# A four-block transformer kernel on one core: three moves in a hand-written order of work

## What is computed

```
x = x + wkv(w, u, layernorm(x), context)          # a recurrence over the rows
x = x + ffn(layernorm(x))                         # 8-bit fake-quantised matmul, relu
x = x + attention(layernorm(x), context)          # 16 heads in 8 groups, self and cross, FP8 inputs
x = x + gated_linear_attention(layernorm(x))      # over the 4 batches
```

```
no  = maximum(o, u + k);      A  = exp(o - no);       E  = exp(u + k - no)
y   = (A * p + E * v) / (A * q + E)
no2 = maximum(w + o, k);      A2 = exp(w + o - no2);  E2 = exp(k - no2)
p, q, o = A2 * p + E2 * v,  A2 * q + E2,  no2
```

## Time and profile before

| | |
|---|---|
| median of 3 runs | 672.46 us (672.37 to 672.68) |
| the profiled execution | 672.11 us, span 670.3 us |
| TensorE matmul | 612.7 us busy, 91% |
| TensorE weight loads | 490.7 us, 73% (beside the matmuls) |
| VectorE | 531.5 us, 79% |
| ScalarE | 398.0 us, 59% |
| GpSimd | 256.2 us, 38% |
| mean granted TensorE clock | 0.985 |
| chain that ended last | TensorE 63%, VectorE 20%, issue 7%, GpSimd 5%, ScalarE 4% |

### The profile page before, as it was taken

How to read it: one execution, slowest core, us unless ns; L and a number is a source line. 1 busy time by engine, 2 the same in 40 slices (tenths; PEclk the granted TensorE clock), 3 DMA queues, 4 the chain that set the end, 5 groups by cost and what they waited for, 6 DMA issues and landing times.

```text
span 670.3 us, 13297 instructions
## 1 busy us (share of the span) xinstructions
PE 612.7 (91%) x4567; PEld 490.7 (73%) x4567; DVE 531.5 (79%) x1305; ACT 398.0 (59%) x1339; POOL 256.2 (38%) x338
## 2 busy tenths in 40 slices
PE   4446999999999999999999999999999999999936
PEld 3345787777778787777788877877888888877725
DVE  7998687988887778888777788888664677868697
ACT  4255766666877545667566456575663665554531
POOL 2115664444333544343344443333332444430233
PEclk9997999999999999999999999999999999999978
DMA  8237452442592202322343232232353234020001
GB/s 266 88 151 200 169 166 56 126 156 89 180 334 100 96 22 102 104 103 106 104 124 99 92 103 103 104 104 103 103 168 100 103 103 103 17 33 1 1 0 63
DMA packets 36973, 72.86 MB, mean 109 GB/s; under 512 B 3343, under 2 KB 28587, under 8 KB 32811
## 3 DMA queue, kind: packets, MB, share of 16 engines
q1 hardware_dynamic: 36720, 72.00, 33.4%
q10 hardware_dynamic: 186, 0.02, 0.0%
HBM read 59.41 MB, written 12.60 MB: 107 GB/s over the span
## 4 chain that ended last, share of the span: by engine, by line
PE 63%; DVE 20%; issue 7%; POOL 5%; ACT 4%; DMA 0%; DVEq 0%; POOLq 0%
PE bank L722 13%; PE bank L702 11%; PE bank L591 10%; PE bank L598 6%; PE bank L674 5%; PE bank L746 3%; PE bank L688 3%; PE bank L703 3%; POOL rs L1343 2%; ACT square L1087 2%; DVE nm L1760 2%; DVE Cb L1775 2%; PE bank L832 2%; PE bank L736 1%; PE bank L841 1%
## 5 line engine op out<-in xcount | busy, mean ns | idle before, releaser
L722 PEld LDWEIGHTS bank<-V,Pt 128*128 128x128 f32 x1024 | 128.1, 191 | 28.7 <-DVE Cb L1775 14.9
L1087 ACT ACTIVATE square<-bank 128x128 bf16<-128x128 f32 x372 | 97.9, 280 | 83.8 <-PE bank L591 70.2
L722 PE MATMUL bank<-V,Pt 128*128 128x129 f32 x1024 | 136.3, 276 | 3.0 <-DVE Cb L1775 2.8
L702 PE MATMUL bank<-QT,KTt 128*128 128x512 f32 x256 | 132.6, 599 | 2.2 <-POOL diag L1358 2.2
L1358 POOL TENSOR_TENSOR diag<-identb,nm 128x512 bf16<-128x512 bf16 x64 | 66.9, 1045 | 174.0 <-DVE nm L1760 173.9
L1070 ACT ACTIVATE Pt<-bank 128x512 f32<-128x512 f32 x128 | 76.9, 601 | 64.1 <-PE bank L703 60.9
L1760 DVE TENSOR_REDUCE nm<-bank 128x2 f32<-128x512 f32 x128 | 82.4, 685 | 27.0 <-PE bank L688 26.6
L1343 POOL TENSOR_TENSOR rs<-ve,mhalf 128x6 f32<-128x6 f32 x64 | 90.0, 1406 | 5.3
L1775 DVE SCALAR_TENSOR_TENSOR Cb<-bank,ro,ism 128x128 bf16<-128x128 f32 x256 | 78.1, 347 | 4.5
L591 PE MATMUL bank<-WQ,xq 128*128 128x256 f32 x512 | 79.3, 297 | 1.0 <-DVE xq L1671 1.0
L1087 ACT ACTIVATION_READ_ACCUMULATOR square<-bank 128x1 f32 x372 | 78.1, 210 | 0.0
(11 more groups left out here) (233 smaller groups left out, 1019.8 us busy)
## 6 DMA issues: line engine op xcount, KB each, us to landing
WQ<-wq_split SPq DMA_DIRECT2D x24, 1024.0 KB, 7.8
WH<-wh_split SPq DMA_DIRECT2D x24, 384.0 KB, 8.9
wq_split<-WQ SPq DMA_DIRECT2D x8, 1024.0 KB, 4.5
ism<-smooth_inverse SPq DMA_DIRECT2D x32, 256.0 KB, 6.4
wst<-in_L_xattn_wproj SPq DMA_DIRECT2D x16, 256.0 KB, 4.5
wh_split<-WH SPq DMA_DIRECT2D x8, 384.0 KB, 3.2
wst<-in_L_xattn_wq SPq DMA_DIRECT2D x8, 256.0 KB, 4.6
wst<-in_L_xattn_wqx SPq DMA_DIRECT2D x8, 256.0 KB, 4.8
```

What stands on the lines that cost most here:

```text
L702: nc.tensor.matmul(o[:], KTt[u % 2][:, x, t * P:(t + 1) * P], QT[u % 2][:, x, :], start=True, stop=False)
L722: last = nc.tensor.matmul(o[:, h * (P + 2):h * (P + 2) + P + 1], Pt[:, x, k, h * S + t * P:h * S + (t + 1) * P], V[u % 2][:, x, k, 0:P + 1 ...
L1087: last = A(square[:, t, h], head(t, h), ACT.Square, accum_out=ss[:, t, h:h + 1])
```

## The change

1. VectorE: the two products that make `no` leave `early(b, 1)` and become a step of their own, -1, behind outputs(u, 0, 0) and ahead of normalise(u + 1, 1). It acts in units 0, 8 and 16.
2. TensorE: turn_z of batches 2 and 3 stands behind guard(u + 1, 1) and no longer ahead of it. It acts in units 12 and 20 (in these no weights are transposed at this place).
3. GpSimd: the last output term is a function of its own. For batch 1 it is issued in unit 2 behind diagonals(2, 0), and no longer at the end of unit 1. For batches 2 and 3 it stays where it was.

```
+        SECOND_OF_1 = -1
...
                 if 0 in steps:
                     turn_h(nb)
-                if 6 in steps and b:
-                    turn_z(nb)
                 if u + 1 != G:
                     for r in round_of(u, 2):
                         weights(*r)
                 guard(u + 1, 1)
+                if 6 in steps and b:
+                    turn_z(nb)
...
                 gp.tensor_tensor(E2, E2, Ew, ALU.add).then_inc(s["den_ready"], 1)
                 chain.wait()
+
+            def last_output_term(b):
+
                 gp.tensor_tensor(A2, Aw, PX[:, :, 0:S], ALU.mult).then_inc(s["ap_ready"], 1)
...
                 diagonals(u, 0)
+                if 3 in steps and u < G:
+                    last_output_term(nb)
...
                 if 2 in steps:
                     output_terms(nb)
+                    if u >= G:
+                        last_output_term(nb)
...
                     last.then_inc(s["wkv_o_ready"], 1)
+                if step == SECOND_OF_1:
                     ch.wait()
                     dve.wait_ge(s["wkv_o_ready"], b)
...
                 outputs(u, 0, 0)
+                if 1 in steps:
+                    early(nb, SECOND_OF_1)
                 normalise(u + 1, 1)
```

## The result

The change makes the kernel slower by half a per cent: the median is 675.80 us (6 runs, 674.26 to 675.98) against 672.29 for the kernel before (6 runs, 672.08 to 672.68), a ratio of 1.0045 with a 95% interval of 1.0035 to 1.0055, or +3.5 us. The forecast was 674.5, in a range of 671.2 to 675.8, so the measured time lies on the upper edge of the range, and outside the 673.4 to 675.6 that the forecast gave its own case. The six executions lie at two levels, two near 674.3 and four near 675.8; that turns out to be the part that the forecast lacked.

The account below looks back on a forecast made before the run. TensorE was taken to bound the units, mostly waiting for VectorE to scale the previous output. The edits' +3.0 − 0.95 − 0.08 = +2.0 us on 672.46 gave 674.5 us, range 671.2 to 675.8.

Parts of the forecast that it names:

- turn(1) ... +2.16: Unit 0, TensorE: the moved products delay normalise, so turn(1) starts at 78.52 for 76.36, 2.16 us later.
- I take 0.5 off: +1.65: Unit 0: TensorE's slack behind turn(1), waits for ScalarE's keys, absorbs 0.5 us of the delay, leaving +1.65 us.
- The sum of edit 1: Moved products in units 0, 8 and 16: 1.65 + 2 × 0.68 = +3.0 us.
- +0.68: Units 8 and 16: turn(9) waits longer for normalise behind the stretched products, +0.68 us in each unit.
- (a): Products of `no`: VectorE is not overtaken between them; the whole change −1.1 us, 671.4; chance 0.18.
- (b): Products overtaken in one kind of unit only: unit 0 672.4, or units 8 and 16 673.5; chance 0.10.
- (c): Products meet no collision, as GpSimd's differences might move with VectorE; −2.0 us, 670.5; chance 0.12.
- −0.95: Units 12 and 20: guard ahead of turn_z fills TensorE's wait, −0.47 us twice, −0.95 in all.
- the bound of −0.5: Units 12 and 20: the largest gain allowed per unit for moving turn_z, −0.5 us; the other bound was 0.
- −0.08: Unit 2: scores start about 1.1 us earlier, but weigh(2,0,1) still waits for outputs; only −0.08 us arrives.
- the forecast's +2.0: Whole kernel: the three edits sum to +3.0 − 0.95 − 0.08 = +2.0 us.
- Rival (e): VectorE's products beside GpSimd: the port lock lasts whole instructions, 1.7 us more, 676.2; chance 0.06.

Follow-up runs that it names:

- unit 0 alone: Only the two products of `no` moved, and only in unit 0, against the kernel before: 674.52 us, ratio 1.0041.
- the filled kernel: The whole change plus fourteen unused identity transposes on TensorE ahead of turn(1) in unit 0; rerun 674.28 us, ratio 1.0029 against the kernel before.

## Why the prediction was right, and where it fell short

**Direction and mechanism: right.** The change is slower, by edit 1, because GpSimd comes in between the two products. The pairs last 2.53 and 2.03; the forecast wanted over 2 in unit 0 and a second product stretched to over 1.3 in unit 8 (1.49). That this collision is the cause is shown by the kernel in which GpSimd's second difference waits.

**Unit 0, "turn(1) ... +2.16": exact; "I take 0.5 off: +1.65": a little too much.** From the reciprocal turn(1) moved from 2.09 to 4.25, +2.16. The slack behind it gave 0.37, not 0.5: +1.79 in the profile of unit 0 alone.

**The term that was missing.** The sum of edit 1 counted what TensorE waits, and took for granted that behind the wait it runs as before. In most executions it does not: after 2.00 us of waiting it runs at 1.2 GHz from 79.5 to 83, and that costs 1.64. The forecast put that at nothing and gave no reason: it said nothing of the granted clock, though the delay of 2.16 that it forecast is the longest that it puts on TensorE anywhere, and the earlier trace rows show no wait over 1.4 for outputs. Edit 1 is then 1.79 + 1.64 + 2 × 0.68 = 4.8, where the forecast had 3.0 and the kernel with edit 1 alone measured 5.05. The forecast's 674.5 is the level without the fall: the filled kernel measures 674.28.

**Units 8 and 16, "+0.68": exact.** Turn(9) comes 0.63 later, and weigh(8, 1, 1) 0.68; unit 16 gives the same. The kernel that moves only these measured 1.2 for both. So rivals (a), (b) and (c) are out: both kinds of unit collide.

**Edit 2, "−0.95": right in kind, too small.** The step to the scores is −0.47 alone and −0.46 with the other edits (4.26 to 3.80), as forecast. But turn(14) then loses its own wait too, and by the end of unit 13 it is −0.60 and −0.58, beyond the bound of −0.5. Both units give −1.2 in either trace; the median of the kernel with edit 2 alone shows −0.84. The power that VectorE waited for came early enough, as argued, and by more than was counted on.

**Edit 3, "−0.08": nothing** that these runs can tell. The reason held: of the 1.11 in front of the scores all but nothing arrives, and the wait for outputs takes its place.

**The sum.** In the trace of after it is 0.18 (head of the program) + 3.43 (unit 0) + 2 × 0.68 − 2 × 0.58 = 3.8, and the span grew by 3.8. The medians give 3.5, since the profiled execution of the kernel before, 672.11, lies 0.18 below its median, and that of after, 675.88, 0.08 above. With the clock's term the forecast's +2.0 becomes +3.6, as the median of six executions of which four have the fall is an execution with the fall.

**What was luck.** Without the fall the units take 2.02 longer (539.21 for 537.19 in the filled kernel), which is the forecast's +2.0 almost exactly. Two errors cancel there: unit 0 was put 0.14 too low, and edit 2's gain 0.2 too low. And the median lies exactly on the upper edge of the range. The clock's term, 1.64, is larger than the distance from the forecast to that edge, 1.3, and the edge was not drawn with the clock in mind; had edit 2 given only its −0.95, the time would have been outside.

**Rival (e)**, that the lock lasts whole instructions, gave 676.2, which is nearer to 675.8 than the forecast is. It is near by accident. Its extra 1.7 was to be in VectorE's pairs, which would have been longer than 2.53 and 2.03; these came out as forecast, with the last product ending 0.27 behind GpSimd's operation, less than a product's 0.48. The Trainium skill (SBUF — State Buffer, SBUF: two separate sides) says that the first of the two engines to start gets the shared ports for the whole instruction and the other fully blocks. The trace agrees that one blocks the other. It also shows the product through 0.27 behind GpSimd's end, so released some 0.2 us before that end, as far as the profile's times of GpSimd are exact.

**What stays open** is why the same 2.00 us are followed by a fall in one execution and not in another: in the change 2 of 6 and then 2 of 5 executions lie at or near the lower level, with unit 0 alone 3 of 5. One difference is to be seen in the traces. The clock's slow stretch at the head of the program ends at about 62.5 in the three traces that have the fall (granted clock 0.69, 0.69 and 0.67 from 60 to 64), and the wait begins 14.0 to 14.4 us later (76.70 in the kernel after); in the one without it, that stretch ends at about 63.8 (0.52) and the wait begins 13.2 us later (77.02). Whether this decides was not tested.

Only one execution of each run has a trace, so for the others the fall is inferred. Two things speak for it: the 1.5 us between the levels, and the mean granted clock of each execution. In the first six of the change it is 0.985 in the two executions near 674.3, and 0.982, 0.982, 0.982 and 0.959 in the four near 675.8; in the nine of the filled kernel it is 0.985 or 0.964. It is a sign and no proof. The later five of the change have 0.962 and 0.959 at 674.37 and 674.87, and 0.982, 0.982 and 0.960 above; with unit 0 alone 674.52 has 0.982. Slow stretches at the head and the end of the program move this mean too: the trace of the kernel with the output term alone has 0.962 and no fall in unit 0.

## What to carry to other kernels

Before an operation is put elsewhere in an engine's order, look at what the other engine of the shared ports does at the new place: here 0.88 us of VectorE work became 2.53 in unit 0, and in units 8 and 16 the move lost 0.68 each, where two places further back it gained 0.95 each. When a forecast puts a new wait on TensorE, price what it does after the wait too, and read the granted clock beside the busy share. A wait removed in front of one instruction counts only if the next thing that the same engine waits for moves as well; the output term moved 1.11 us of waiting and gained nothing.

## What the runs showed of the hardware that was not expected

- A single wait of 2.00 us, in a stretch in which TensorE is otherwise almost wholly busy, was followed by about 3.4 us at 1.2 GHz in three of four traces, at a cost of 1.64 us. Waits of 1.41 (unit 8) and 0.98 (unit 0, second difference held back) were not. With 1.70 us of transposes in the wait, which change nothing else, 12 of 13 executions lay between 673.75 and 674.71, and one at 675.18, with a mean granted clock of 0.959.
- The length of the wait does not decide alone: the same 2.00 us left the granted clock at 1.00 in the profile with unit 0 alone. The fall gives a kernel two levels of time 1.5 us apart, and a median that depends on how often each is met. A few runs can then differ by more than either level's own spread.
- Between two products that VectorE issues back to back, a waiting GpSimd operation came in at every such boundary of these traces, in units 0, 8 and 16 alike: the second product took 1.31 us in the kernel before and 1.48 to 1.50 in the kernels with the edit, for 0.48.
- One execution of 2200.83 us among those of 674: no cause of it was looked for.
